# SyncE's programs of three stages written out straight instead of in loops

## What is computed

```python
x = _layernorm(x + _L0_gnn_ref(x, L0_gnn_W, L0_gnn_b, edge_index), axis=-1)
x = _layernorm(x + _L1_gnn_ref(x, edge_index, L1_gnn_W1, ...), axis=-1)
# L0: per edge relu([x_i, x_j - x_i] @ W + b), then the maximum over the edges of a node
# L1: coefficients from column means; five times tx = segment_sum(norm * tx[col], row)
```

## Time and profile before

| | us |
|---|---|
| median of three runs | 3424.88 |
| lowest and highest | 3422.96, 3433.43 |
| the profiled execution, its own time | 3425.53 |
| its span (first to last instruction) | 3423.8 |

### The profile page before, as it was taken

The page is one execution under the profiler, slowest core; times in us unless marked ns, Lnnn a source line. Parts: engine busy times, 40 slices in busy tenths (PEclk is TensorE's granted clock), DMA queues, the critical chain, the costliest instruction groups (busy, mean ns, idle before and its releaser), DMA issues. The chain is left out here.

```text
span 3423.8 us, 69227 instructions
## 1 busy us (share of the span) xinstructions
PE 1943.0 (57%) x9465; PEld 1136.4 (33%) x9465; DVE 2587.5 (76%) x12088; ACT 2064.9 (60%) x5029; POOL 2194.8 (64%) x2359
## 2 busy tenths in 40 slices
PE   6998555387778875988988988333432333000000
PEld 4776444244444543444444444111111111000000
DVE  7998999998988985777878787645656666555554
ACT  6998888367666763777777777425554600344443
POOL 5665666266666665666667666466765666677776
PEclk9999999799999996677677676555555555555555
DMA  3301444266666664677777777566766733222221
GB/s 118 116 22 37 112 105 108 53 171 188 186 183 183 187 180 117 160 183 177 179 179 186 183 181 169 153 149 167 204 177 164 198 97 77 70 72 69 72 74 53
DMA packets 736768, 467.17 MB, mean 136 GB/s; under 512 B 411287, under 2 KB 622546, under 8 KB 736728
## 3 DMA queue, kind: packets, MB, share of 16 engines
q1 hardware_dynamic: 636084, 321.23, 34.4%
q0 software_dynamic: 75296, 92.22, 12.7%
q10 hardware_dynamic: 25348, 53.33, 4.9%
HBM read 271.38 MB, written 197.86 MB: 137 GB/s over the span
## 5 line engine op out<-in xcount | busy, mean ns | idle before, releaser
L976 POOL DMA_INDIRECT rec<-rec_sb,pos x392 | 395.6, 1009 | 236.8 <-issue 228.0
L1686 POOL DMA_INDIRECT rows_H<-tab,at_H x424 | 408.2, 963 | 211.7 <-DVE at_H L1750 110.7
L1177 POOL DMA_INDIRECT rows_M<-x_ext,at_M x400 | 380.2, 951 | 194.3 <-issue 188.8
L1966 POOL DMA_INDIRECT out_x<-res_L,to_L x384 | 373.8, 973 | 139.8 <-issue 100.8
L1718 ACT ACTIVATE node_H<-node_H,mean,M2n 125x64 f32<-125x64 f32 x800 | 273.6, 426 | 256.8 <-issue 150.4
L1858 PE MATMUL zT_H<-ident,z_H 128*64 128x128 f32 x496 | 150.5, 408 | 443.2 <-issue 347.9
L876 PE MATMUL gps<-table,hiT 125*128 125x400 bf16 x1568 | 311.2, 343 | 85.0 <-DVE picked L810 83.9
L394 POOL DMA_INDIRECT rows_x<-in_x,at_x x196 | 190.6, 973 | 118.3 <-issue 68.8
L553 POOL DMA_INDIRECT rows_y<-in_x,at_y x196 | 188.2, 960 | 118.0 <-ACT edge_x L580 64.3
L787 DVE SCALAR_TENSOR_TENSOR eq<-srcbc,recs,mask 128x128 bf16<-128x128 f32 (+3 forms) x392 | 194.6, 551 | 65.8 <-DMA srcbc<-src_rows 65.5
L1983 ACT ACTIVATE std_L<-M_L,coef 128x2 f32<-128x2 f32 x192 | 56.7, 296 | 284.4 <-DVE M_L L2045 284.2
(11 more groups left out here) (327 smaller groups left out, 6280.2 us busy)
## 6 DMA issues: line engine op xcount, KB each, us to landing
tab<-given_M SPq DMA_DIRECT2D x98, 384.0 KB
hibc_f<-dst_hi_rows SPq DMA_DIRECT2D x98, 256.0 KB
hibc<-hi_rows SPq DMA_DIRECT2D x98, 256.0 KB
srcbc<-src_rows SPq DMA_DIRECT2D x98, 256.0 KB
tab<-given_M SPq DMA_DIRECT2D x98, 256.0 KB
own<-given_M SPq DMA_DIRECT2D x98, 256.0 KB
own_L<-own SPq DMA_DIRECT2D x192, 128.0 KB
x_ext<-wide SPq DMA_DIRECT2D x100, 241.5 KB
```

The lines of the kernel that those rows point to most:

```text
L976: pool.indirect_dma_start(out=d.rec, out_offset=bass.IndirectOffsetOnAxis(ap=pos[:, s, j:j + 1], axis=0), in_=rec[:, s, j, :], in_offset=N ...
L1177: pool.indirect_dma_start(out=rows[:, s, j, :], out_offset=None, in_=d.x_ext, in_offset=bass.IndirectOffsetOnAxis(ap=at[:, s, j:j + 1], ax ...
L1686: pool.indirect_dma_start(out=rows[:, s, j, :], out_offset=None, in_=gather, in_offset=bass.IndirectOffsetOnAxis(ap=at[:, s, j:j + 1], axi ...
L1966: pool.indirect_dma_start(out=d.out, out_offset=bass.IndirectOffsetOnAxis(ap=to[:, s, j:j + 1], axis=0), in_=res[:, s, j, :], in_offset=No ...
```

## The change

`settle` returns at once when all its values are plain numbers, so no register work and no wait on `k.begun` is made for them. SyncE's loop of the placing stage becomes a Python loop, its `pipeline` of the edge pass becomes `written_out` (same steps, same order, every period written out), and its two loops of the result stage become 47 rounds written out and a loop for the one to three that are left. The first two of the 47 have fixed places; the place of the others is computed from the loaded numbers by `place`, one formula for the near and the other rounds.

```diff
--- before.py
+++ after.py
@@ -117,6 +117,8 @@
+    if values and all(isinstance(v, int) for v in values):
+        return values
     for v in values:
         eng.lower_val(v)
     eng.wait_ge(k.begun, 1)
@@ -759,7 +761,7 @@
                 rows(1, 1)
                 widened(0, 1)
                 widen(1, 0)
-                with sp.Fori(1, LAST) as i:
+                for i in range(1, LAST):
                     rows(i + 1, 0)
                     widened(i, 0)
                     widen(i, 1)
@@ -1031,6 +1033,14 @@
+def written_out(groups, ns, *steps):
+
+    for t in range(groups + max(lag for lag, _, _ in steps)):
+        for lag, last, step in steps:
+            if 0 <= t - lag <= last:
+                step((t - lag) // ns, (t - lag) % ns)
@@ -1162,7 +1172,7 @@
-            pipeline(sp, NG, NS, (0, NG - 1, load_ids), (1, NG - 1, load_chunk), (2, LAST, load_x), (8, LAST, give))
+            written_out(NG, NS, (0, NG - 1, load_ids), (1, NG - 1, load_chunk), (2, LAST, load_x), (8, LAST, give))
@@ -1945,14 +1955,22 @@
             n, (first, gap) = rounds(sp), rounds_here(sp, k)
-            with sp.Fori(0, n) as i:
-                at = near_round(i, first, gap)
+            end = rounds_end(sp)
+
+            def place(r):
+                near = r + ((r + (128 - first)) >> 7) * gap
+                other = r - n + first + ((r + (128 - n - gap)) >> 7) * (n - first)
+                return (near + ((r + (128 - n)) >> 7) * (other - near)).with_bounds(min_val=0, max_val=ROUNDS - 1)
+
+            sure = ROUNDS - LATE - 1
+            for r in range(sure):
+                at = r if r < 2 else place(r)
                 for s in range(NS):
-                    load(i, at, s)
-            with sp.Fori(0, rounds_other(sp)) as i:
-                at = other_round(i, first, gap, n)
+                    load(r, at, s)
+            with sp.Fori(0, end - sure) as i:
+                at = place(i + sure)
                 for s in range(NS):
-                    load(i + n, at, s)
+                    load(i + sure, at, s)
```

## The result

| | before | after |
|---|---|---|
| median of 20 runs, us | 3430.36 | 3421.72 |
| lowest and highest | 3422.54, 3435.57 | 3409.90, 3432.73 |
| the profiled execution, us | 3425.53 | 3425.51 |
| its span, us | 3423.8 | 3423.8 |

The changed kernel takes 0.9976 of the time, with a 95% interval of 0.9965 to 0.9986: 8.6 us less, where 21 us were forecast. By the bound of 0.3% this is no change, though the interval leaves out zero. The two profiled executions are equally long by chance; that of after is one of its slower ones. So I go by stages, and the length of a stage is read between two marks inside it.

The account below looks back on a forecast made before the run. The placing stage was taken as bound by a ring through SyncE's row load: 33 rings x 0.65 us = -21.5 us, +1 us code loading, 0 elsewhere, from 3425.5 to 3405 us; as a median 3404 us, range 3385 to 3429 us.

Parts of the forecast that it names:

- What bounds the kernel: Placing stage: some 33 rings of three tiles, 19.4 us each, with SyncE's time from `wide` to row load fully on them.
- The passage: Placing stage: SyncE's time from the end of `wide` to the load of rows becomes 0.81 us shorter in the mean.
- How much arrives: Placing stage: of the 0.81 us saved, 0.50 to 0.81 us a ring is gained, 0.65 us taken.
- Rival 1: Placing stage: transfers set the landing, earlier issues only queue longer; 0 to 8 us gained, 3417 to 3425 us; chance 0.20.
- Rival 3: Placing stage: loads brought forward delay the scatters' landing, at 1.1 us making it 15 us slower, 3440 us; chance 0.07.
- Rival 2: Placing stage: shorter passages make the late tile vanish in some rings; 28 to 50 us gained, 3375 to 3396 us; chance 0.10.
- The sum: Whole kernel: -21.5 us placing stage, +1 us code loading, 0 edge pass, 0 result stage, about -21 us.
- Rival 4: Edge pass: a denser placing stage lowers TensorE's clock, costing 23 us, or 39 us giving 3442 us; chance 0.05.
- Code loading: Whole kernel: loading 1,803 more instructions costs 1 us, 6 us if every 128 instructions cost 0.4 us.
- Edge pass and result stage: Both later stages: SyncE's savings are covered by its own waits; 0 each, with 5 us either way for the edge pass.

Follow-up runs that it names:

- place_alone: Kernel before with only SyncE's loop of the placing stage written out, edge pass and result stage still loops; 0.9978 of the time before.
- small_straight: Changed kernel with SyncE's column loads of the placing stage moving one column of eight from tile 2 on; 0.9873 of the time before, stage 602.4 us.
- delay_front: Changed kernel with a loop of three waiting turns, 0.77 us, ahead of SyncE's two stores in the placing stage; 1.0034 of the time before.
- edge_alone: Kernel before with only SyncE's program of the edge pass written out; 0.9982 of the time before.
- result_alone: Kernel before with only SyncE's two loops of the result stage replaced as in the change; 1.0000 of the time before.
- rows_first: Changed kernel with the placing stage's load of rows of tile n + 3 issued ahead of the wait for `wide` of tile n; 0.9792 of the time before.
- rows_first_place: Kernel before with the row load ahead of the wait for `wide` and only the placing stage written out; 0.9793 of the time before.
- rows_between: Changed kernel with the placing stage's load of rows put between the stores and the column load; 1.0265 of the time before, stage 729.9 us.
- delay_short: Changed kernel with a loop of three waiting turns, 0.77 us, ahead of each load of rows in the placing stage; 0.9968 of the time before.
- delay_long: Changed kernel with a loop of seven waiting turns, some 1.75 us, ahead of each load of rows in the placing stage; 1.0045 of the time before.

## Why the prediction was wrong

**What bounds the kernel.** This was right: a ring through `wide`, SyncE's queue and the row load, over three tiles, and with it the sign. The path has 30 such rings where the prediction had 33. The reading had a gap: `pos` at 952.83 is not that of the tile ranked at 950.93, but of tile 40. VectorE's order closes the ring all the same. That "37 waits over 98 tiles" gave nearly the right count was in part luck; the changed kernel has 43 waits and the same 30 rings.

**The passage.** Shorter by 0.68 us and by 0.19 us in front of it: 0.87 us for 0.81 forecast. The issues took as long as before. All this held.

**How much arrives.** This is the step that failed. The bounds were 0.50 to 0.81 us a ring; by the stage lengths 7.5 / 30 = 0.25 us arrived. Two landings on the ring grew. That of the rows grew by 0.46 us in after and 0.37 us in place_alone (0.47 and 0.44 us a ring on the path). The argument for the bounds was that the DMA engines were not full (0.75) and that the column loads leave sooner. But the column loads' packets go first, and small_straight shows that without most of them the rows' landing does not grow. That of the scatters, put at nothing in the forecast, grew by 0.31 and 0.24 us a ring on the path.

**Rival 1** had the first of these mechanisms. It was right for the part of the saving that lies behind the stores, and not for the part in front, which arrives for the most part (delay_front). Its time, 3417 to 3425 us, holds 3421.7 us by some luck: it was counted from 3424.9 us, and the kernel before had 3430.4 us beside the changed one, so the 8.6 us lie just over its 0 to 8 us.

**Rival 3** shows in part: the scatters land later (2.67 us before, 2.67 and 2.71 us in edge_alone and result_alone, 3.13 and 3.10 us in after and place_alone), and ScalarE's wait for them rose from 120.0 to 145.0 us. It took away gain; it did not make the stage slower. Why they land later is open: denser issues alone do not explain it, since delay_front has them as dense and 2.76 us. **Rival 2** did not come about.

**The sum.** 33 x 0.65 = 21.5 us should have been 30 x 0.87 = 26 us, less some 14 us for the rows' landing and some 7 to 9 us for the scatters'. By these terms 3 to 5 us are left; measured were 7.5 us in the stage, with some 3 us to either side, and 8.6 us by the medians. The wait for `srcbc` should have fallen to 44 us and fell to 60.0 us.

**Rival 4**, a lower clock, did not come about: it is 0.69 in both profiled edge passes. In the timed runs it was the other way round. The mean clock of the whole span was 0.729 in the 20 runs of after and in the 12 of place_alone, and 0.725 in the 33 of before beside place_alone (the 20 of before in the result have no clock on record). Within one kernel's runs 0.001 of the clock goes with 1.3 to 1.6 us, so by this estimate some 5 of the 8.6 us could be the clock's. The profiled stages speak for the placing stage (4.3 and 9.9 us shorter than that of before); how much of the medians' difference each has is not told apart.

**Code loading** was put at 1 us. The passages are 1.96 us in the mean, just what the straight rows gave, so none shows there. Over the kernel the queue that loads instructions moved 48 packets for 34. The rule of the Trainium skill ("Runtime: NRT & Kernel Launch", Instruction fetch mechanics) that the prediction cites, that crossing a block is mostly hidden, agrees with this.

**Edge pass and result stage** were put at 0. The result stage was that (1.0000). For the edge pass edge_alone alone says 0.18%; rows_first against rows_first_place show nothing, nor do the kernels that make SyncE slower there by 1.5 us a period, over twice the 0.57 us that the change saves. I hold the 0.18% for the clock's doing (0.728 in the mean of edge_alone's runs, 0.725 in those of before beside them), but that is argued, not shown.

## What to carry to other kernels

Follow a ring by tile number and by the order of each engine's list: a wait on an engine that executes in order is passed on to whatever stands behind it, of another tile too. Two ranks of different tiles made one tight ring here, and the tile numbers alone gave a wrong one over five tiles. Before counting an earlier DMA issue as an earlier landing, look at what stands in front of it in the same queue, and at what else on the ring lands beside it: here 0.77 us between the column loads and the rows cost some 5 us of the stage, and 20 us ahead of the first store. And where a load waits behind somebody else's wait in an in-order program, try the order before the instructions: turned, it gave 2%, and writing the program out then gave nothing; but note each other ring that the new order lengthens, as rows_between did by 16%.

## What the runs showed of the hardware

**Landing of a load depends on how close its forerunners are, at a share under one.** With 250 KB of column loads in front, the row pair landed 4.97 us after its issue when the passage took 1.96 us, 4.51 us at 2.64 and at 2.73 us, and 4.27 us at 3.73 us. The difference lies ahead of the first row packets, which start 1.33 us after the issue before and 1.74 us after. With 31 KB in front it was 4.5 us at both 1.74 and 2.50 us.

**The timing of SyncE's transfers moves the landing of GpSimd's scatters.** The last landing of a tile's four scatters came 2.67 to 2.71 us after the fourth in three kernels with the loop of before (before, edge_alone, result_alone), and 3.13 and 3.10 us with it written out (after, place_alone). With the written-out loop and delays it was 3.00 us in delay_short, 2.76 us in delay_front and 2.63 us in delay_long.

**The edge pass has two lengths.** In 15 executions without a delay of SyncE there, it took 837.0 to 838.2 us four times, at a clock of 0.71 or 0.72, and 843.5 to 848.9 us eleven times, at 0.68 to 0.70, with nothing between. Both forms of SyncE's program show both: three of nine written out and one of six looped were short. The means of the two lie 8.5 us apart, over a third of the 23 us between the changed kernel's lowest and highest run, and effects under 0.2% are hard to get at beside them.

**Holding SyncE up raised TensorE's clock.** With 1.5 us more a period the clock was granted at 0.77 in place of 0.69, between the two levels of 1.2 and 2.4 GHz (0.50 and 1.00), and the pass took 837.3 us, the short length; so it did, 837.4 and 837.6 us, in the two kernels of turned order. What TensorE did differently before a rise of the clock was not looked into. At 3.0 us a period the clock was 0.67 and the pass took 875.5 us.
